# DLRM interaction tower on one core: rounds of sums over six units instead of four, with the dense features summed by TensorE

## The chip, the cores and the metric

The kernel runs on one core of one Trainium2 chip. The metric is the device time of an execution in microseconds (us).

## The reference, cut to what matters

512 examples look up one row of 64 floats in each of 40 tables. Each of the 780 pairs of fields has a 64 x 64 matrix, and gives one number per example. These 780 numbers and 16 dense features go through a small network.

```python
e = jnp.stack([tbl_0[ids[:, 0]], ..., tbl_39[ids[:, 39]]], axis=1)        # (512, 40, 64)
vi, vj = e[:, i_idx, :], e[:, j_idx, :]                                   # all pairs i < j, 780 of them
z = jnp.einsum('bpe,bpe->bp', jnp.einsum('bpd,pde->bpe', vi, W), vj)      # (512, 780)
h = jnp.concatenate([z, dense_ctx], axis=1)                               # (512, 796)
h = jnp.maximum(h @ W_top1 + b_top1, 0.0)                                 # 512 wide
h = jnp.maximum(h @ W_top2 + b_top2, 0.0)                                 # 256 wide
y = h @ W_top3
```

## The kernel before, in words

Everything is float32. The fields are kept in 20 pairs (NP), a pair on the 128 partitions of `x[:, k, :]`, 512 examples on the free axis. Sixteen pairs are gathered by GpSimd's indirect transfers (line 308) and turned by TensorE into bank `t_ps` (line 447, a "turn"); four pairs of small tables are looked up by TensorE with one-hot rows (line 429) that VectorE makes (line 385). ScalarE copies either into `x` (line 321).

The pairs of fields are worked through in 195 units (lines 64 to 74): 190 cross units (pair m with pair k, four matrices) and 5 inner units. For each unit s, in this order:

- TensorE (`multiply`, line 460) multiplies the unit's matrices with `x` into one of three slots of `y_ps` (Y_SLOTS; each slot is two banks): lines 477 for a cross unit, two products of 64 rows each, which run beside each other, and 483 for an inner one. It waits until VectorE has finished unit s - 3 (line 465). Each float32 matmul shows as two records.
- VectorE (`multiply`, line 394) multiplies both banks with the other pair of fields into `prod`, 128 x 1024 in one instruction (line 407). `prod` holds twelve units (G_UNITS); VectorE waits until the round that reads the old ones is done (line 396).
- TensorE (`sum_round`, line 488) sums the products over the 64 partitions of each half, and so makes rows of z: one matmul with a moved window of `selector` for each of a unit's two products, into one 32-partition quarter of the bank `z_ps` (line 500). Matmuls on different quarters run beside each other. A round takes ROUND = 4 units, eight products, two on each quarter, and is issued SUM_LAG = 3 units after its last unit. So the order on TensorE is: four units, a round, four units, a round. It waits for VectorE's last product of the round.
- After BANK_ROUNDS = 8 rounds `z_ps` is full with 128 rows (four more a round on each quarter) and ScalarE copies it to `z_sb` (line 337). There are seven such banks; the last gets one round of three units (`LAST_UNITS`).

Between the units stand jobs whose places are planned (`plan_jobs`, line 110): the turn of pair k goes three units before its first use, and two partial products of the first layer with banks 0 and 1, then 2 and 3 (line 456), four matmul groups each, spaced by six units and placed relative to ROUND and BANK_ROUNDS (line 120). All use the one bank `t_ps`. VectorE's one-hot rows for the last look-up are made at units 4, 7, 10 and 13 (ROWS_AT, line 47).

At the end TensorE begins the first layer with bank 4 (line 508), sums the last round, and goes on with banks 4, 5 and 6. The dense features are loaded early by a transfer straight into rows 4 to 19 of the last bank of `z_sb` (line 274; the rest of it is zeroed by VectorE at line 368), so ScalarE copies the last round in three pieces of four rows, one for each quarter in use (line 353), and leaves those rows standing. The second layer (line 538) and the last (line 544) follow.

SP issues the chunks of eight units' matrices, held back by the progress of the units (line 248), GpSimd's gathers are paced by it too (line 307).

Of the kernel before, what the change touches and what calls it, by code (L numbers as in the profile page):

```python
# [8 lines left out]
ACT = mybir.ActivationFunctionType  # L9
# [9 lines left out]
N_DENSE = 16  # L19
# [12 lines left out]
Y_SLOTS = 3  # L32
G_UNITS = 12
ROW_SLOTS = 6
ROUND = 4
BANK_ROUNDS = 8
SUM_LAG = 3
MIX_SLOTS = 2
LEAD = 3
# [38 lines left out]
STEPS = len(UNITS)  # L78
CHUNKS = -(-STEPS // CHUNK)
ROUNDS = -(-STEPS // ROUND)  # L80
BANKS = -(-ROUNDS // BANK_ROUNDS)
LAST_UNITS = STEPS - ROUND * BANK_ROUNDS * (BANKS - 1)
assert LAST_UNITS <= ROUND and STEPS == 195
FIRST_LATE = 2 * PARTIAL_PAIRS
DENSE_ROW = 4
INNER_AT = {u[1]: s for s, u in enumerate(UNITS) if u[0] == "inner"}


def pairs_of(s):

    unit = UNITS[s]
    if unit[0] == "cross":
        _, m, k = unit
        return [(h, h, hh, 2 * m + h, 2 * k + hh) for h in range(2) for hh in range(2)]
    a = 4 * unit[1]
    return [(n % 2, n // 2, n % 2 ^ n // 2, 2 * (a + n) + n % 2, 2 * (a + n) + 1 - n % 2) for n in range(4)]
# [5 lines left out]
    return slice(D * at, D * at + D)  # L102


def z_row(s, bank, half):
    r = s // ROUND
    return r // BANK_ROUNDS, 32 * (s % ROUND) + 4 * (r % BANK_ROUNDS) + 2 * bank + half


def plan_jobs():  # L110
# [8 lines left out]
    for pair in range(PARTIAL_PAIRS):  # L119
        start = ROUND * BANK_ROUNDS * 2 * (pair + 1) + SUM_LAG + 4  # L120
        for m in range(M1):
# [16 lines left out]
def round_at(s):  # L138
    r, rest = divmod(s - SUM_LAG - (ROUND - 1), ROUND)
    return r if rest == 0 and r >= 0 else None  # L140


def dlrm_tower(nc, ids, ids_one_hot, row_numbers, small_tables, tables, dense_t, w_units, w1, b1, w2, b2, w3, out):
    ctx = ExitStack()
    with ctx:
        def sb(name, shape, dt=F32):
            return ctx.enter_context(nc.sbuf_tensor(name, shape, dt))

        def ps(name, shape):
            return ctx.enter_context(nc.psum_tensor(name, shape, F32))  # L150

        def sem(name):
            return ctx.enter_context(nc.semaphore(name))

        ids_sb = sb("ids_sb", [P, BT, F], I32)
        ident = sb("ident", [P, P])
        selector = sb("selector", [P, 62])
# [5 lines left out]
        prod = sb("prod", [P, 2 * G_UNITS, B])  # L163
        z_sb = sb("z_sb", [P, BANKS, B])
# [22 lines left out]
        z_ps = ps("z_ps", [P, B])  # L187
        t_ps = ps("t_ps", [P, B])[:]

        def turn_ps(n):  # L190
            bank = TURN_BANK[n]
            return t_ps if bank == 2 * Y_SLOTS else y_ps[:, bank // 2, bank % 2, :]
# [13 lines left out]
        dense_loaded = sem("dense_loaded")  # L206
# [14 lines left out]
        round_summed = sem("round_summed")  # L221
        z_saved = sem("z_saved")
# [15 lines left out]
        def wait_x(eng, k):  # L238
            wait_turn_done(eng, TURN_SEQ["look" if k in ONE_HOT_PAIRS else "turn", k])
# [4 lines left out]
        def _(sp):  # L244
# [25 lines left out]
            for c in range(1, CHUNKS):  # L270
                load_weights(c)
                if c == 5:
                    sp.wait_ge(z_zeroed, 1)
                    sp.dma_start(z_sb[DENSE_ROW:DENSE_ROW + N_DENSE, BANKS - 1, :],
                                 dense_t).then_inc(dense_loaded, 16)
# [37 lines left out]
        @block.scalar  # L313
        def _(act):
            def copy_turn(job):
                n = TURN_SEQ[job]
                if job[0] == "partial" and job[1]:
                    return
                act.wait_ge(turned, n + 1)
                if job[0] in ("look", "turn"):  # L320
                    act.activation(x[:, job[1], :], turn_ps(n), ACT.Copy).then_inc(turn_on_act, 1)  # L321
                else:
                    act.activation(partial[job[2]], turn_ps(n), ACT.Copy).then_inc(turn_on_act, 1)

            def mix(q):
                if q >= MIX_SLOTS:
                    act.wait_ge(prod_ready, INNER_AT[q - MIX_SLOTS] + 1)
                for n in range(4):

                    k, into, other = 4 * q + n, D * (n % 2 ^ n // 2), D * (1 - n % 2)  # L330
                    wait_x(act, k)
                    act.activation(x_mix[into:into + D, q % MIX_SLOTS, n // 2, :], x[other:other + D, k, :],  # L332
                                   ACT.Copy).then_inc(mixed, 1)

            def save_bank(r):
                act.wait_ge(round_summed, r + 1)
                act.activation(z_sb[:, r // BANK_ROUNDS, :], z_ps[:], ACT.Copy).then_inc(z_saved, 1)  # L337

            for s in range(STEPS):
                for job in JOBS_AT[s]:  # L340
                    if job[0] == "mix":
                        mix(job[1])
                    else:
                        copy_turn(job)
                if (r := round_at(s)) is not None and r % BANK_ROUNDS == BANK_ROUNDS - 1:
                    save_bank(r)
            for r in range(BANK_ROUNDS - 1, ROUNDS, BANK_ROUNDS):
                if ROUND * r + ROUND - 1 + SUM_LAG >= STEPS:
                    save_bank(r)
            act.wait_ge(round_summed, ROUNDS)  # L350
            act.wait_ge(dense_loaded, 16)
            for c in range(LAST_UNITS):
                act.activation(z_sb[32 * c:32 * c + 4, BANKS - 1, :], z_ps[32 * c:32 * c + 4, :],
                               ACT.Copy).then_inc(z_saved, 1)
            act.wait_ge(mlp_loaded, 64)
            for m in range(M1):
                act.wait_ge(h1_added, m + 1)
                act.activation(h1_sb[:, m, :], partial[m], ACT.Relu, bias=b1_sb[:, m:m + 1]).then_inc(h1_ready, 1)
            for m in range(M2):
                act.wait_ge(h2_summed, m + 1)  # L360
                act.activation(h2_sb[:, m, :], h2_ps[m], ACT.Relu, bias=b2_sb[:, m:m + 1]).then_inc(h2_ready, 1)
            act.wait_ge(out_summed, 1)
            act.activation(y_sb, out_ps, ACT.Copy).then_inc(out_ready, 1)  # L363
# [57 lines left out]
        def _(pe):  # L421
# [66 lines left out]
            def sum_round(r):  # L488
                units = range(ROUND * r, min(ROUND * r + ROUND, STEPS))
                pe.wait_ge(prod_ready, units[-1] + 1)  # L490
                if r == 0:
                    pe.wait_ge(selector_ready, 2)
                elif r % BANK_ROUNDS == 0:
                    pe.wait_ge(z_saved, r // BANK_ROUNDS)
                row = 4 * (r % BANK_ROUNDS)
                for n in range(2):
                    for u in units:
                        last = n == 1 and (r % BANK_ROUNDS == BANK_ROUNDS - 1 or u + ROUND >= STEPS)
                        q = 32 * (u % ROUND)
                        ins = pe.matmul(z_ps[q:q + 32, :], selector[:, 30 - row - 2 * n:62 - row - 2 * n],  # L500
                                        prod[:, 2 * (u % G_UNITS) + n, :],
                                        start=(n == 0 and row == 0), stop=last)
                ins.then_inc(round_summed, 1)

            def first_layer(b, m):
                if m == 0:
                    pe.wait_ge(z_saved, b + 1 if b < BANKS - 1 else b + LAST_UNITS)
                return pe.matmul(h1_ps[m], w1_sb[:, b, P * m:P * m + P], z_sb[:, b, :],  # L508
                                 start=(b == FIRST_LATE), stop=(b == BANKS - 1))

            pe.wait_ge(ident_ready, 1)
            for s in range(STEPS):
                for job in JOBS_AT[s]:
                    if job[0] != "mix":
                        turn(job)
                multiply(s)
                if (r := round_at(s)) is not None:
                    sum_round(r)
# [10 lines left out]
            for b in range(FIRST_LATE, BANKS):  # L529
                for m in range(2 if b == FIRST_LATE else 0, M1):  # L530
                    ins = first_layer(b, m)
# [3 lines left out]
            for k in range(M1):  # L535
                pe.wait_ge(h1_ready, k + 1)
                for m in range(M2):
                    ins = pe.matmul(h2_ps[m], w2_sb[:, k, P * m:P * m + P], h1_sb[:, k, :],  # L538
                                    start=(k == 0), stop=(k == M1 - 1))
                    if k == M1 - 1:  # L540
                        ins.then_inc(h2_summed, 1)
            for k in range(M2):
                pe.wait_ge(h2_ready, k + 1)
                ins = pe.matmul(out_ps, w3_sb[:, k:k + 1], h2_sb[:, k, :], start=(k == 0), stop=(k == M2 - 1))  # L544
# [3 lines left out]
def pair_numbers():  # L548
    return {p: n for n, p in enumerate(zip(*np.triu_indices(F, k=1)))}
# [13 lines left out]
def lay_out_top1(w):  # L563
    number = pair_numbers()
    laid = np.zeros((P, BANKS, N1), w.dtype)
    for s in range(STEPS):
        for _, bank, half, i, j in pairs_of(s):
            z_bank, row = z_row(s, bank, half)
            i, j = ORDER[i], ORDER[j]
            laid[row, z_bank] = w[number[(min(i, j), max(i, j))]]  # L570
    laid[DENSE_ROW:DENSE_ROW + N_DENSE, BANKS - 1] = w[len(number):]
    return laid


# [35 lines left out]
```

## Time and profile before

| | |
|---|---|
| median of 3 runs | 365.91 us (365.79 to 366.19) |
| the profiled execution: its own time | 367.68 us |
| the profiled execution: span | 365.9 us |
| TensorE matmuls busy | 349.1 us (95%) |
| VectorE busy | 259.1 us (71%) |
| GpSimd busy | 153.9 us (42%) |
| ScalarE busy | 38.4 us (10%) |
| TensorE on the chain that ended last | 87% |

The span runs from the first to the last instruction in the trace. PE is TensorE's matmul, PEld its weight load, DVE VectorE, ACT ScalarE, SP SyncE. The chain of waits is followed back from the last instruction, at each step to what released it. L500 is line 500 of the kernel.

### The profile page before, as it was taken

What the parts mean: (1) busy time and instruction counts of PE and PEld (TensorE: products, weight loads), DVE (VectorE), ACT (ScalarE), POOL (GpSimd) and SP (SyncE); (2) the same over time, 40 slices, a digit from 0 to 9 for tenths busy, and PEclk for the clock granted to TensorE, in tenths of its full rate; (3) what the DMA queues carried; (4) which work ended last, traced back from release to release, by engine and by line L of the source; (5) the groups of instructions that cost most, each with busy time, mean ns of one, the idle gap of its engine ahead of it and who ended that gap; (6) DMA issues with size and microseconds to landing.
All of it is one profiled execution on the core that took longest, in us unless ns stands there. A gap on an engine that the chain in (4) does not pass through costs nothing.

```text
span 365.9 us, 4723 instructions
## 1 busy us (share of the span) xinstructions
PE 349.1 (95%) x1848; PEld 118.1 (32%) x1848; DVE 259.1 (71%) x271; ACT 38.4 (10%) x61; POOL 153.9 (42%) x261
## 2 busy tenths in 40 slices
PE   0989979999999999999999999999999999999997
PEld 0332223333323333333333333333333333333342
DVE  3956688378787787665768787887668687877430
ACT  1010300030100301010000300000000001200232
POOL 2888888337776754443534453253223000000000
PEclk9999989999999999999999999999999999999999
DMA  6961122002722222112202221122022000000000
GB/s 205 409 246 22 23 79 75 20 14 73 277 83 64 92 77 72 59 22 73 68 11 73 72 69 23 58 71 68 13 65 68 5 0 2 0 0 3 0 1 0
DMA packets 11448, 24.29 MB, mean 66 GB/s; under 512 B 3857, under 2 KB 3857, under 8 KB 11298
## 3 DMA queue, kind: packets, MB, share of 16 engines
q1 hardware_dynamic: 7330, 19.79, 15.4%
q0 software_dynamic: 4096, 4.20, 5.5%
q8 instruction: 14, 0.23, 0.3%
q14 instruction: 8, 0.07, 0.1%
HBM read 23.98 MB, written 0.00 MB: 66 GB/s over the span
## 4 chain that ended last, share of the span: by engine, by line
PE 87%; issue 8%; DVE 2%; DMA 1%; ACT 1%; SPq 0%; DVEq 0%
PE y_ps L477 45%; PE z_ps L500 24%; PE t_ps L456 4%; PE y_ps L508 3%; PE t_ps L447 2%; PE t_ps L429 2%; PE y_ps L429 2%; PE y_ps L538 2%; DVE one_hot L385 1%; DMA x<-in_ids_one_hot 1%; PE y_ps L483 1%; DVE prod L407 1%; ACT x L321 1%; PE t_ps L544 0%; ACT prod L363 0%
## 5 line engine op out<-in xcount | busy, mean ns | idle before, releaser
L407 DVE TENSOR_TENSOR prod<-y_ps,x 128x1024 f32<-128x1024 f32 x190 | 221.0, 1217 | 75.7 <-PE y_ps L477 74.4
L477 PE MATMUL y_ps<-x,w_sb 64*128 64x512 f32 x760 | 182.5, 610 | 4.9 <-ACT x L321 2.3
L308 POOL DMA_INDIRECT rows<-in_tbl,ids_sb x128 | 122.7, 958 | 129.6 <-PE y_ps L477 92.7
L477 PEld LDWEIGHTS y_ps<-x,w_sb 64*128 64x128 f32 x760 | 67.0, 186 | 109.3 <-issue 58.2
L500 PE MATMUL z_ps<-prod,selector 128*32 128x512 f32 x780 | 95.3, 604 | 0.0
L500 PEld LDWEIGHTS z_ps<-prod,selector 128*32 128x32 f32 x780 | 20.6, 110 | 67.9 <-issue 37.7
L429 PE MATMUL t_ps<-one_hot,table 128*64 128x512 f32 x96 | 22.8, 631 | 8.4 <-DVE one_hot L385 8.4
L385 DVE TENSOR_SCALAR one_hot<-x,numbers 128x512 f32<-128x512 int32 x64 | 27.2, 496 | 4.9 <-DMA x<-in_ids_one_hot 4.9
L303 POOL MEMSET spacer<- 128x128 f32 x127 | 30.5, 240 | 0.1
L321 ACT ACTIVATE x<-t_ps 128x512 f32<-128x512 f32 x18 | 10.8, 597 | 188.8 <-PE t_ps L447 149.9
L456 PE MATMUL t_ps<-z_sb,w_sb 128*128 128x512 f32 x32 | 15.9, 618 | 0.0
L429 PEld LDWEIGHTS t_ps<-one_hot,table 128*64 128x64 f32 x96 | 7.2, 146 | 22.8 <-issue 22.5
L332 ACT ACTIVATE x_mix<-x 64x512 f32<-64x512 f32 x20 | 12.6, 628 | 0.5
L337 ACT ACTIVATE z_sb<-z_ps 128x512 f32<-128x512 f32 x6 | 3.6, 597 | 80.5 <-PE z_ps L500 80.5
L508 PE MATMUL y_ps<-z_sb,w_sb 128*128 128x512 f32 x24 | 10.8, 601 | 0.0
L447 PE MATMUL t_ps<-ident,rows 128*128 128x128 f32 x60 | 9.8, 286 | 0.7 <-ACT x L321 0.7
L447 PEld LDWEIGHTS t_ps<-ident,rows 128*128 128x128 f32 x60 | 6.3, 140 | 12.8 <-issue 9.7
L418 DVE TENSOR_TENSOR partial_sb<-y_ps,partial_sb 128x512 f32<-128x512 f32 x3 | 2.1, 691 | 10.0 <-PE y_ps L508 10.0
L456 PEld LDWEIGHTS t_ps<-z_sb,w_sb 128*128 128x128 f32 x32 | 5.4, 189 | 10.2 <-issue 10.2
L429 PE MATMUL y_ps<-one_hot,table 128*64 128x512 f32 x32 | 7.0, 592 | 0.0
L538 PE MATMUL y_ps<-prod,w_sb 128*128 128x512 f32 x16 | 7.0, 592 | 0.0
L407 DVE TENSOR_TENSOR prod<-y_ps,x_mix 128x1024 f32<-128x1024 f32 x5 | 6.1, 1217 | 0.9 <-issue 0.9
(30 smaller groups left out, 36.1 us busy)
## 6 DMA issues: line engine op xcount, KB each, us to landing
w_sb<-in_w_units SPq DMA_DIRECT2D x25, 512.0 KB
x<-in_ids_one_hot SPq DMA_DIRECT2D x8, 256.0 KB, 4.9
table<-in_small_tables SPq DMA_DIRECT2D x8, 256.0 KB, 4.8
rows<-in_tbl,ids_sb POOLq DMA_INDIRECT x128
w_sb<-in_w SPq DMA_DIRECT2D x1, 1792.0 KB
w_sb<-in_w SPq DMA_DIRECT2D x1, 512.0 KB
ids_sb<-in_ids SPq DMA_DIRECT2D x1, 80.0 KB, 4.7
z_sb<-in_dense_t SPq DMA_DIRECT2D x1, 32.0 KB
```

Source lines behind the costliest of these rows:

```text
L303: pool.memset(spacer[:], 0.0).then_inc(spaced, 1)
L308: pool.indirect_dma_start(rows[:, n % ROW_SLOTS, bt, h * D:(h + 1) * D], None, tables[f], bass.IndirectOffsetOnAxis(ap=ids_sb[:, bt, f:f + ...
L321: act.activation(x[:, job[1], :], turn_ps(n), ACT.Copy).then_inc(turn_on_act, 1)
L385: ins = dve.tensor_scalar(one_hot[:, h, k, :], ids_all[:, 2 * n + h, :], numbers[:, k:k + 1], None, ALU.is_equal)
L407: dve.tensor_tensor(prod[:, at:at + 2, :], y_ps[:, s % Y_SLOTS], leaf, ALU.mult).then_inc(prod_ready, 1)
L429: ins = pe.matmul(dst[D * h:D * h + D, :], table[:, n, h, k, :], one_hot[:, h, k, :], start=(k == 0), stop=(k == TK - 1))
L447: ins = pe.transpose(dst[:, P * bt:P * bt + P], rows[:, at % ROW_SLOTS, bt, :], ident[:])
L456: ins = pe.matmul(dst, w1_sb[:, b, P * m:P * m + P], z_sb[:, b, :], start=(b % 2 == 0), stop=(b % 2 == 1))
L477: ins = pe.matmul(y_ps[:, slot, h, :], w_sb[own, c % W_SLOTS, at:at + P], x[own, m, :], start=True, stop=True)
L500: ins = pe.matmul(z_ps[q:q + 32, :], selector[:, 30 - row - 2 * n:62 - row - 2 * n], prod[:, 2 * (u % G_UNITS) + n, :], start=(n == 0 and ...
L508: return pe.matmul(h1_ps[m], w1_sb[:, b, P * m:P * m + P], z_sb[:, b, :], start=(b == FIRST_LATE), stop=(b == BANKS - 1))
L538: ins = pe.matmul(h2_ps[m], w2_sb[:, k, P * m:P * m + P], h1_sb[:, k, :], start=(k == 0), stop=(k == M1 - 1))
```

## The change

A round takes six units, twelve products, laid one after the other on the four quarters in three turns, each turn two rows further. A bank takes five rounds (120 rows), there are still seven banks, and 33 rounds in place of 49. The last round has three units. Its bank is now copied whole; the dense features, still loaded into `z_sb` (now rows 16 to 31), are first added into `z_ps`, on quarter 2, rows 16 to 31 of it, by one more matmul with 32 columns of the identity. The partials move from units 71, 77, 83, 89 and 135, 141, 147, 153 to 67, 73, 79, 85 and 127, 133, 139, 145. Y_SLOTS, G_UNITS and SUM_LAG stay. With ROUND = 6, the order on TensorE is six units, a round, six units, a round.

```diff
-ROUND = 4
-BANK_ROUNDS = 8
+ROUND = 6
+BANK_ROUNDS = 5
+QUARTERS = 4
+ROUND_ROWS = 4 * ROUND // QUARTERS
...
-LAST_UNITS = STEPS - ROUND * BANK_ROUNDS * (BANKS - 1)
-assert LAST_UNITS <= ROUND and STEPS == 195
+LAST_UNITS = STEPS - ROUND * (ROUNDS - 1)
+assert LAST_UNITS == 3 and STEPS == 195
...
-DENSE_ROW = 4
+
+DENSE_ROW = 16
+DENSE_QUARTER = 2 * LAST_UNITS % QUARTERS
...
+def place_of(u, bank):
+
+    return divmod(2 * u + bank, QUARTERS)
+
+
 def z_row(s, bank, half):
     r = s // ROUND
-    return r // BANK_ROUNDS, 32 * (s % ROUND) + 4 * (r % BANK_ROUNDS) + 2 * bank + half
+    turn, quarter = place_of(s % ROUND, bank)
+    return r // BANK_ROUNDS, 32 * quarter + ROUND_ROWS * (r % BANK_ROUNDS) + 2 * turn + half
...
-            act.wait_ge(round_summed, ROUNDS)
-            act.wait_ge(dense_loaded, 16)
-            for c in range(LAST_UNITS):
-                act.activation(z_sb[32 * c:32 * c + 4, BANKS - 1, :], z_ps[32 * c:32 * c + 4, :],
-                               ACT.Copy).then_inc(z_saved, 1)
+            save_bank(ROUNDS - 1)
...
-                row = 4 * (r % BANK_ROUNDS)
-                for n in range(2):
-                    for u in units:
-                        last = n == 1 and (r % BANK_ROUNDS == BANK_ROUNDS - 1 or u + ROUND >= STEPS)
-                        q = 32 * (u % ROUND)
-                        ins = pe.matmul(z_ps[q:q + 32, :], selector[:, 30 - row - 2 * n:62 - row - 2 * n],
-                                        prod[:, 2 * (u % G_UNITS) + n, :],
-                                        start=(n == 0 and row == 0), stop=last)
+                row = ROUND_ROWS * (r % BANK_ROUNDS)
+                for u in units:
+                    for n in range(2):
+                        turn, quarter = place_of(u % ROUND, n)
+                        first = row + 2 * turn
+                        if r == ROUNDS - 1:
+                            last = 2 * (u % ROUND) + n + QUARTERS > 2 * LAST_UNITS
+                        else:
+                            last = r % BANK_ROUNDS == BANK_ROUNDS - 1 and turn == 2 * ROUND // QUARTERS - 1
+                        ins = pe.matmul(z_ps[32 * quarter:32 * quarter + 32, :], selector[:, 30 - first:62 - first],
+                                        prod[:, 2 * (u % G_UNITS) + n, :], start=(first == 0), stop=last)
+                if r == ROUNDS - 1:
+                    pe.wait_ge(dense_loaded, 16)
+                    ins = pe.matmul(z_ps[32 * DENSE_QUARTER:32 * DENSE_QUARTER + 32, :], ident[:, 0:32],
+                                    z_sb[:, BANKS - 1, :], start=False, stop=True)
                 ins.then_inc(round_summed, 1)
 
             def first_layer(b, m):
                 if m == 0:
-                    pe.wait_ge(z_saved, b + 1 if b < BANKS - 1 else b + LAST_UNITS)
+                    pe.wait_ge(z_saved, b + 1)
```

The rows of the first layer's weights are laid out on the host to match.

## Rows read from the trace of the kernel before

**Rows 1.** Busy time by stretch: stretch, length, PE, PEld, DVE, ACT, POOL, PEclk, DMA.

```profile
48.70:52.50 3.80, 3.80 (x16) 0.87 (x20) 3.80 (x7) 0.00 (x0) 2.99 (x6) 0.55 0.10 17
...
69.09:342.48 273.39, 273.36 (x1537) 91.98 (x1537) 210.23 (x183) 23.19 (x38) 102.58 (x175) 1.00 0.18 53
```

**Rows 2.** Chain of waits, middle: start us, us, engine, tile, line, records.

```profile
192.44 3.63 PE y_ps L477 x16
196.08 1.85 PE z_ps L500 x16
...
226.32 1.92 PE y_ps L477 x8
228.24 0.58 PE t_ps L447 x4
...
249.06 1.91 PE t_ps L456 x4
...
308.09 1.06 PE y_ps L477 x4
```

**Rows 3.** Timeline, 161 to 169 us: start, us, engine, line, records, [idle before <-releaser].

```profile
161.24 1.13 PE L477 MATMUL y_ps<-x,w_sb 64*128 64x512 f32 x4
...
165.80 3.70 PE L477 MATMUL y_ps<-x,w_sb 64*128 64x512 f32 x16
...
167.05 4.62 DVE L407 TENSOR_TENSOR prod<-y_ps,x 128x1024 f32<-128x1024 f32 x4 [1.69 <-PE y_ps L477]
...
168.33 0.35 PEld L477 LDWEIGHTS y_ps<-x,w_sb 64*128 64x128 f32 x4 [0.51 <-DVE prod L407]
```

**Rows 4.** Timeline, 113 to 121 us, where VectorE is behind.

```profile
113.04 8.01 DVE L407 TENSOR_TENSOR prod<-y_ps,x 128x1024 f32<-128x1024 f32 x7 [1.65 <-PE y_ps L477]
...
115.05 3.79 PE L477 MATMUL y_ps<-x,w_sb 64*128 64x512 f32 x16
...
117.71 0.30 PEld L477 LDWEIGHTS y_ps<-x,w_sb 64*128 64x128 f32 x4 [0.64 <-DVE prod L407]
```

**Rows 5.** Timelines of PE, then of DVE, 40 to 70 us.

```profile
40.76 1.09 PE L483 MATMUL y_ps<-x,w_sb 64*64 64x512 f32 x8
41.78 1.93 PE L500 MATMUL z_ps<-prod,selector 128*32 128x512 f32 x16
43.64 3.31 PE L477 MATMUL y_ps<-x,w_sb 64*128 64x512 f32 x12
48.68 1.70 PE L477 MATMUL y_ps<-x,w_sb 64*128 64x512 f32 x4 [1.74 <-DVE prod L407]
50.30 3.00 PE L500 MATMUL z_ps<-prod,selector 128*32 128x512 f32 x16
...
61.22 7.09 PE L429 MATMUL t_ps<-one_hot,table 128*64 128x512 f32 x32
69.09 1.13 PE L477 MATMUL y_ps<-x,w_sb 64*128 64x512 f32 x4 [0.79 <-ACT x L321]
...
42.28 2.34 DVE L407 TENSOR_TENSOR prod<-y_ps,x 128x1024 f32<-128x1024 f32 x2
...
47.41 3.47 DVE L407 TENSOR_TENSOR prod<-y_ps,x 128x1024 f32<-128x1024 f32 x3
...
52.44 1.20 DVE L407 TENSOR_TENSOR prod<-y_ps,x 128x1024 f32<-128x1024 f32 x1
55.90 2.36 DVE L407 TENSOR_TENSOR prod<-y_ps,x 128x1024 f32<-128x1024 f32 x2 [2.26 <-PE y_ps L477]
58.18 1.78 DVE L385 TENSOR_SCALAR one_hot<-x,numbers 128x512 f32<-128x512 int32 x4
```

**Rows 6.** Chain of waits at the end.

```profile
344.39 1.85 PE z_ps L500 x12
346.24 8.78 PE y_ps L508 x20
```

**Rows 7.** Groups of instructions on ScalarE: busy us, mean ns, idle before.

```profile
L353 ACT ACTIVATE z_sb<-z_ps 4x512 f32<-4x512 f32 x3 | 1.8, 587 | 3.2 <-PE z_ps L500 3.2
```

More of the change, by code:

```diff
@@ L570, in lay_out_top1 @@
             laid[row, z_bank] = w[number[(min(i, j), max(i, j))]]
-    laid[DENSE_ROW:DENSE_ROW + N_DENSE, BANKS - 1] = w[len(number):]
+    dense_row = 32 * DENSE_QUARTER + DENSE_ROW
+    laid[dense_row:dense_row + N_DENSE, BANKS - 1] = w[len(number):]
     return laid
```

## The prediction, made before the changed kernel ran

> **What bounds the kernel now.** I read the stages first [rows 1]. From 69.09 us to 342.48 us TensorE has no gap: 273.36 of 273.39 us busy at granted clock 1.00, the higher of its two levels (2.4 GHz), while VectorE works 210.23 us. So this middle, three quarters of the time, is TensorE's. Then the chain of waits [rows 2]: it stays on TensorE and falls into pieces of a few fixed lengths. Units in a run: 1.06 us for one, 1.92 for two, 3.63 for four, so 0.857 us each, and the first of a run 0.205 more. A round of sums over four units (two turns of four quarters) takes 1.85 us: two turns of 0.855 (two passes at the pace of the units' passes) and 0.14 fixed. A turn of gathered rows takes 0.58 to 0.59, a partial first layer 1.91 to 1.92. Last, how close VectorE stands behind it [rows 3]: its first product starts 1.25 us after the first weight load of a run (165.80 to 167.05), it takes 1.22 us, and four end 4.62 us after the first began, so they follow each other by 1.13. TensorE's load for the run's fourth unit went at 168.33, 0.06 after that first product had ended (168.27): there are only three y_ps slots. From a load to the end of its unit's matmuls are 1.13 us (the run of one unit). The fourth unit would by itself end 3.70 after the start and can end at 2.53 + 1.13 = 3.66 by the slot: four units fit with 0.04 to spare. That margin is the whole case.
>
> **Rounds and restarts.** 49 rounds become 33; in the middle stretch, where order and counts follow from the planner, 45 become 30. A round of twelve products in three turns takes 0.14 + 3 x 0.855 = 2.705 us. The turns set it, not the products: the last round, with twelve records on three quarters, took 1.85 as the sixteen on four did [rows 6, 2]. 45 x 1.85 = 83.25 becomes 30 x 2.705 = 81.15: 2.10 less. Runs of cross units (each ended by a round, a turn, a partial or an inner unit) fall from 60 to 52, as many of the new ones are still cut by a job: 8 x 0.205 = 1.64 less. As a check, the old counts (175 cross units at 0.857, 60 restarts, 4 inner units at 1.02, 13 turns, 8 partials, 45 rounds) give 272.6 us against 273.4 in the trace; the rest is a few late VectorE starts, which I leave in. Sum: **3.74 us less** if nothing waits.
>
> The fixed 0.14 and 0.205 are where a mode of TensorE changes. The Trainium skill ("TensorEngine Tiling (Array Packing)", Key Properties) says that changing the tiling mode drains the engine; by that rule fewer rounds are a plain gain. The same page (PSUM Bottleneck) warns that tiling speeds up TensorE but not the emptying of PSUM, which may become the bottleneck. That speaks against this change, and the next step is its case in rows.
>
> **The wait that comes.** Six units now follow each other. From the first load of the run, and with VectorE idle as it is there: units 0 to 3 end at 1.13, 1.99, 2.84, 3.70. VectorE starts at 1.25, 2.39, 3.52, 4.65 and ends 1.22 later: 2.47, 3.61, 4.74. The load of unit 4 waits for the second product: 3.67, and the unit ends at 4.80, not 4.56 (0.24 late). Unit 5 waits for the third: load at 4.80, end at 5.93. By itself it would end at 5.41: **0.515 us lost per uninterrupted six**. The round behind takes 2.705, VectorE is through at about 8.15, the next run starts at 8.56, so nothing carries over and each such run pays again. That this is how a late slot is paid the trace shows once [rows 4]: seven products back to back (8.01 us), a weight load at 117.71, 0.06 after a product, and the run ends at 118.84, 1.13 behind the load, 0.09 later than four units by themselves. By the order of the new plan the middle has 11 uninterrupted sixes (5.67), three runs of five cross units (0.24 each) and three bursts where an inner unit sits within the six (0.15 each): **6.83 us more**. The other bursts are cut after at most four units by a turn (with the restart 0.8 us) or a partial (2.1), in which VectorE catches up; those cost nothing. VectorE's fresh idle time is not work and costs nothing by itself. Bounds of this term: 5.7 (each uninterrupted six 0.1 us cheaper, twice the 0.04 to 0.06 to which rows 3 fix a step) to 7.6 (the 0.75 us of late starts met once more, in runs without slack).
>
> **The beginning** [rows 5]. Here VectorE's one-hot rows are on the chain. Before, round 0 (41.78) stands ahead of unit 7, whose slot was free only at 43.55 anyway; units 7, 8, 9 end at 46.94, and TensorE then waits 1.74 us for a product. Round 1 comes at 50.30, at a lowered clock, before turn and unit 11, and so VectorE's unit 11 starts only at 55.90 after 2.26 us of idleness. After: units 7 and 8 end at 45.9, round 0 (2.7) fills the wait, unit 9 ends at 49.6 against 48.5 to 49.7 that VectorE wants; unit 10 at 50.5, the turn at 51.1 (it waited for no gather before, at 53.23), and unit 11 can start at 51.8, behind the copy of that turn (some 0.78 us, as before unit 16 at 69.09). VectorE's unit 11 then follows unit 10 directly at 53.6, its one-hot rows of step 13 (from 58.18 before) are done by 57.6, and units 13 to 15 and round 1 end by 59.7. The look-up starts at 59.6 instead of 61.22, unit 16 at 67.5 instead of 69.09: **1.6 us less**. The clock is the doubt: it was 0.55 from 48.7 to 52.5 [rows 1], behind the 1.74 us of waiting [rows 5], and stretched round 1 from 1.93 to 3.00 and unit 10 from 1.13 to 1.70. After, TensorE waits as long, but from 41.85 (the inner unit's end) to 43.55, and is then dense. If it falls all the same it lands on round 0 and unit 9, delays them by some 1.5 us and the gain is gone. Bounds: 0 to 2.1 less. I take 1.6, as what comes right behind the wait is now denser.
>
> **The end.** The last round has six products and the dense one, on quarters 0, 1, 2, 3, 0, 1 and 2: two turns, 1.85 us as before [rows 6]. Should the dense product not run beside the others, 0.86 more; I take 0. ScalarE's three copies of 4 rows (0.587 us each, [rows 7]) become one; they lay beside the first layer's twelve passes ahead of bank 6 (some 5.1 of the 8.78 us, [rows 6]), so 0 again. Cover gone, they would have cost 1.8. The dense wait is for a transfer issued near the sixth weight chunk, over long before. Partials move 4 to 8 units forward; w1 has landed long before, bank 1 is copied five units ahead. ScalarE and the SP and POOL queues issue the same, paced by the same units. Products have twelve slots: unit 12 needs round 0, which is issued behind unit 8, so VectorE doesn't wait there.
>
> **Sum:** -3.74 + 6.83 - 1.6 = +1.5 us. The profiled execution has a span of 365.9 us and its own time was 367.68; I set the change against its span and put it on the median of the runs, 365.91: 367.4. A measurement of this kernel can tell about 0.2% (0.73 us) from no change.
>
> **The rivals.**
> (a) The clock falls in the beginning again: +3.1, 369.0. For it: the same length of waiting. Against: the round now stands right behind. 0.2.
> (b) The other side, faster: the run of six doesn't wait, since the load for unit 4 and 5 overlaps the product before it or VectorE starts each run earlier. Then -3.74 - 1.6: 360.6. It decides where the waits sum to less than 4.6 us of my 6.83. Against it stand rows 3 and 4, where load follows product by 0.06 and end follows load by 1.13. By the drain rule of the Trainium skill ("TensorEngine Tiling (Array Packing)", Key Properties) alone this would be the result. 0.1.
> (c) The change doesn't do what it says: the third turn isn't as cheap as the second, with another 0.14 or so of start for each of 30 rounds: +4.2 more, 371.6. Rows 2 and 6 give no sign. 0.05.
> (d) Smaller errors in both terms cancel and leave nothing to measure: waits at 5.7 and the beginning at 2.1 give 365.8. 0.1.
> The forecast itself has 0.55, of which 0.04 ends within 0.73 us of no change and 0.02 below.
>
> **How the numbers follow.** Likeliest 367.4. The range leaves out (b), (c) and the edges: from 365.4, just below (d), to 369.8, which is (a) with the waits at 7.6. Slower: the forecast's 0.49, (a) and (c), 0.74. Same: (d) and the forecast's 0.04, 0.14. Faster: (b) and 0.02, 0.12.
>
> **What would show it.** Chain: sum rounds of 24 records at 2.70; runs of six at 5.86 in place of 5.34 (0.52 more), with loads of y_ps released by VectorE at units 4 and 5, 0.06 after a product; runs of four before a partial at 3.63. The idle time of VectorE grows, though its work is the same. Unit 16 at about 67.5 and no stretch at 0.5 clock, or a stretch on round 0, which would be (a). The end from 342 on keeps its 23.4 us. Runs of six at 5.34 would make the prediction wrong toward (b), rounds over 2.8 toward (c).

## The result, and the profile after

The changed kernel takes 370.4 us (median of 6, 369.2 to 371.03), the kernel before 366.05 us beside it (median of 6): ratio 1.0111, interval 1.0089 to 1.0133. It is slower, as forecast, but by 4.35 us where 1.5 were forecast, and it lies outside the range (365.4 to 369.8). One execution of the kernel before, of 1247 us, is left out of everything below.

Its profiled execution has a span of 367.3 us, 1.4 more than that of before. That looks like the forecast and isn't: the two profiles are of different kinds of execution. Either kernel has executions whose granted clock is 1.00 on the mean and others with 0.995. Each profile of the second kind (seven, of these two kernels and of variants) has one stretch at the lower level (1.2 GHz), which lies between 43 and 54 us. The profile of before was of that kind [rows 1], that of after of the first. Over all comparisons of this study in which the span is on record:

| | clock 1.00 | clock 0.995 |
|---|---|---|
| before | 48 executions, mean 364.05 us | 32 executions, mean 365.5 us |
| after | 8 executions, mean 367.8 us | 10 executions, mean 369.65 us |

So the loss is 3.8 us against the same kind at 1.00 and 4.1 at 0.995, and a median also depends on how many executions of each kind it holds. Device time is 1.75 to 2.13 us above the span in all 80 executions of before, and in 16 of the 18 of after; in the other two, both of this first comparison, it is 2.31 and 3.12 above.

Busy time by stretch of the kernel after (columns as in [rows 1]): the middle, from unit 16 to the first layer, and the place where before had its clock stretch.

```profile
67.75:343.94 276.19, 275.90 (x1537) 92.22 (x1537) 208.97 (x183) 23.81 (x39) 102.94 (x177) 1.00 0.16 52
48.70:52.50 3.80, 3.02 (x16) 1.38 (x18) 3.80 (x7) 0.60 (x1) 2.98 (x6) 1.00 0.12 26
```

The middle is 2.8 us longer than the 273.39 of [rows 1]; that one held 0.3 us of late VectorE starts, and the undisturbed middle of before is 273.0 (below). In the experiments the middle ends with the first record of the first layer, 0.07 us earlier than in this line; by that it is 276.12 here. Its chain of waits, to set beside [rows 2]:

```profile
180.04 3.63 PE y_ps L483 x16
183.68 0.59 PE t_ps L453 x4
184.27 1.92 PE y_ps L483 x8
186.18 2.71 PE z_ps L510 x24
...
197.45 4.72 PE y_ps L483 x20
202.17 0.09 issue
202.26 1.13 PE y_ps L483 x4
203.39 2.71 PE z_ps L510 x24
...
242.88 3.63 PE y_ps L483 x16
246.52 1.91 PE t_ps L462 x4
```

A round of twelve products takes 2.71 us, the sum's 2.705. Four units ahead of a turn or a partial take 3.63 here, as before, and up to 3.71 elsewhere. An uninterrupted six takes 4.72 + 0.09 + 1.13 = 5.94 here and in one other place, and 5.84 to 5.88 in nine, where six by themselves would be 5.34. Over the eleven the waits come to 5.7 us, and 5.67 was worked out. The timeline of that run, to set beside [rows 3]:

```profile
197.38 6.01 PE L483 MATMUL y_ps<-x,w_sb 64*128 64x512 f32 x24
...
198.63 5.75 DVE L413 TENSOR_TENSOR prod<-y_ps,x 128x1024 f32<-128x1024 f32 x5 [1.68 <-PE y_ps L483]
...
201.04 0.30 PEld L483 LDWEIGHTS y_ps<-x,w_sb 64*128 64x128 f32 x4 [0.78 <-DVE prod L413]
...
202.23 0.33 PEld L483 LDWEIGHTS y_ps<-x,w_sb 64*128 64x128 f32 x4 [0.89 <-issue]
```

VectorE begins 1.25 us after the first load, as before. The load of unit 4 went at 201.04, 3.66 after the start of the run (3.67 was worked out), and that of unit 5 at 202.23, 4.85 after it (4.80 worked out). The row calls the second gap "issue", but the load goes 0.12 behind the end of the third product (198.63 + 1.22 + 2 x 1.13 = 202.11).

The beginning, to set beside [rows 5]: PE's timeline of the kernel after.

```profile
40.77 1.09 PE L489 MATMUL y_ps<-x,w_sb 64*64 64x512 f32 x8
43.58 2.35 PE L483 MATMUL y_ps<-x,w_sb 64*128 64x512 f32 x8 [1.72 <-DVE prod L413]
45.86 2.78 PE L510 MATMUL z_ps<-prod,selector 128*32 128x512 f32 x24
48.57 1.99 PE L483 MATMUL y_ps<-x,w_sb 64*128 64x512 f32 x8
50.49 0.66 PE L453 MATMUL t_ps<-ident,rows 128*128 128x128 f32 x4
51.92 4.25 PE L483 MATMUL y_ps<-x,w_sb 64*128 64x512 f32 x16 [0.78 <-ACT x L331]
56.10 2.78 PE L510 MATMUL z_ps<-prod,selector 128*32 128x512 f32 x24
58.81 1.13 PE L483 MATMUL y_ps<-x,w_sb 64*128 64x512 f32 x4
59.87 7.09 PE L435 MATMUL t_ps<-one_hot,table 128*64 128x512 f32 x32
```

The wait for VectorE of 1.74 us ahead of unit 10 has become one of 1.72 ahead of unit 7. Units 11 to 14 take 4.18 (51.92 to 56.10) where four take 3.63, as VectorE is still behind. The end (chain of waits), beside [rows 6]:

```profile
343.94 1.91 PE y_ps L521 x4
345.85 1.41 PE z_ps L510 x10
347.26 0.01 PE z_ps L514
347.27 0.42 PE z_ps L510 x2
347.69 0.01 PE z_ps L514
347.70 8.78 PE y_ps L521 x20
```

The last round with the dense product (line 514) takes 1.85 us in sum, as forecast. The dense product's two records show as 0.01 us each: it runs beside the others. From the first layer on, both kernels take 23.4 us.

### The profile page after: what moved, and what is told of

The parts are those of the page before. It is cut to its first block, busy times and chain, and to the rows that moved or that the text cites. A ratio compares the mean times of both kernels' runs of the same rounds, so it can differ in the third digit from the quotient of the medians.

```text
span 367.3 us, 4724 instructions
## 1 busy us (share of the span) xinstructions
PE 350.7 (95%) x1850; PEld 118.3 (32%) x1850; DVE 258.1 (70%) x271; ACT 37.2 (10%) x59; POOL 154.0 (42%) x261
## 4 chain that ended last, share of the span: by engine, by line
PE 90%; POOL 3%; DMA 3%; issue 2%; ACT 1%; DVE 1%; SPq 0%; DVEq 0%
PE y_ps L483 49%; PE z_ps L510 24%; PE t_ps L462 4%; PE t_ps L435 4%; PE y_ps L521 3%; PE t_ps L453 2%; POOL rows L318 2%; PE y_ps L551 2%; DMA rows<-in_tbl,ids_sb 2%; DMA ids_sb<-in_ids 1%; PE y_ps L489 1%; POOL spacer L313 1%; ACT x L331 1%; PE t_ps L557 0%; DVE one_hot L391 0%
## 5 line engine op out<-in xcount | busy, mean ns | idle before, releaser
L483 PE MATMUL y_ps<-x,w_sb 64*128 64x512 f32 x760 | 186.3, 613 | 5.2 <-ACT x L331 2.3
L483 PEld LDWEIGHTS y_ps<-x,w_sb 64*128 64x128 f32 x760 | 65.6, 185 | 115.3 <-issue 61.1
L510 PE MATMUL z_ps<-prod,selector 128*32 128x512 f32 x780 | 90.9, 596 | 0.0
L510 PEld LDWEIGHTS z_ps<-prod,selector 128*32 128x32 f32 x780 | 22.1, 109 | 63.9 <-issue 55.6
```

The costliest lines, as they stand in the source:

```text
L483: ins = pe.matmul(y_ps[:, slot, h, :], w_sb[own, c % W_SLOTS, at:at + P], x[own, m, :], start=True, stop=True)
L510: ins = pe.matmul(z_ps[32 * quarter:32 * quarter + 32, :], selector[:, 30 - first:62 - first], prod[:, 2 * (u % G_UNITS) + n, :], start=(f ...
```

## The experiments

### The kernel before again

No edit.

> The kernel before, unchanged, to see span and clock of each execution. Theory (atypical profile): the profile of before held a clock stretch at 0.5 that most of its executions don't have; then most spans are near 364.0 us at granted clock 1.00, and one with 0.995 is near 365.9. In a profile without the stretch unit 16 starts near 67.5 us in place of 69.09. Rival (the stretch is always there, and the changed kernel loses outside what its profile shows): all spans near 365.9 at 0.995.

Measured: 367.38 us against 366.17 for the runs beside it; ratio 1.0014, interval 0.9997 to 1.003. Spans of its own executions: 363.5, 363.9, 363.9 at clock 1.00 and 365.5 to 365.8 at 0.995, eight times. Of the executions beside it, 17 of 23 were at 1.00. The theory holds in that there are two kinds, 1.5 us apart. That most are of the first kind holds over all (48 of 80) and not in this run's own eleven. Its profile had the stretch again, so the profile without one comes from the next run.

### The new layout and the dense product with rounds of four

```diff
-ROUND = 6
-BANK_ROUNDS = 5
+ROUND = 4
+BANK_ROUNDS = 8
```

> The changed kernel with rounds of four units and eight rounds a bank: only the new laying on the quarters, the dense product in the last round and the whole copy of the last bank are left of the change. Theory: the last round stays at 1.85 us and the time is that of the kernel before within 0.3 us. Rival (the dense product or the copy is on the path): 0.4 to 0.9 us slower, with the last round at 2.3 to 2.7.

Measured: 366.19 us against 366.17, ratio 0.9996, interval 0.9981 to 1.0012. The layout, the dense product and the whole copy cost nothing and bring nothing. As its order of work is that of the kernel before, its profile at clock 1.00 also shows what that of before would have been. PE's timeline and the busy time of the middle:

```profile
41.20 1.09 PE L489 MATMUL y_ps<-x,w_sb 64*64 64x512 f32 x8
42.22 1.92 PE L510 MATMUL z_ps<-prod,selector 128*32 128x512 f32 x16
44.22 3.39 PE L483 MATMUL y_ps<-x,w_sb 64*128 64x512 f32 x12
49.27 1.13 PE L483 MATMUL y_ps<-x,w_sb 64*128 64x512 f32 x4 [1.66 <-DVE prod L413]
50.33 1.92 PE L510 MATMUL z_ps<-prod,selector 128*32 128x512 f32 x16
```

```profile
68.04:341.06 273.02, 272.99 (x1536) 91.97 (x1536) 210.22 (x183) 23.17 (x38) 102.57 (x175) 1.00 0.18 53
```

Unit 10 takes 1.13 and round 1 takes 1.92 us, where [rows 5] have 1.70 and 3.00: 1.65 us less, with nothing changed in the order. Executions begin up to 1 us apart, so I count from the inner unit: unit 16 starts 26.84 us behind it here (68.04 - 41.20), 28.33 in the profile of before (69.09 - 40.76) and 26.98 in that of after (67.75 - 40.77). The changed order itself gains nothing in the beginning; it loses 0.14 us.

### VectorE's products cut to three quarters, before and after

Both kernels with KEPT = 384: VectorE leaves out the products of the last 128 of the 512 examples.

```diff
-dve.tensor_tensor(prod[:, at:at + 2, :], y_ps[:, s % Y_SLOTS], leaf, ALU.mult)
+dve.tensor_tensor(prod[:, at:at + 2, 0:KEPT], y_ps[:, s % Y_SLOTS, :, 0:KEPT], leaf, ALU.mult)
```

> The kernel before with VectorE's products cut to 384 of the 512 examples (the last 128 of prod are zeroed once at the start, so their output is wrong): its pace falls from 1.13 to about 0.87 us a unit, TensorE's work is as before. Theory (VectorE doesn't bind in runs of four): the middle stretch, from unit 16 to the first layer, keeps its 273.4 us within 0.8; in all at most 2 us faster by the beginning. Rival (VectorE already holds back the runs of four): the middle gains over 2 us.

> The changed kernel with the same cut of VectorE's products to 384 of 512 examples (same part of the output wrong). Theory (each uninterrupted run of six waits 0.5 us for a y_ps slot): the waits vanish, runs of six go from 5.84 to 5.34 us, the middle stretch goes from 276.2 to 269 or 270 us, and this kernel is 3 to 4.5 us faster than the kernel before with the same cut, so the sign of the change turns. Rival (the longer run is slow for another reason, on TensorE itself): runs of six stay at 5.8, and it stays 2 to 4 us slower than the kernel before with the cut.

Measured: 363.78 us with rounds of four (ratio to the kernel before 0.9918, interval 0.9897 to 0.9939) and 360.77 us with rounds of six (0.9835, 0.9814 to 0.9856). The middle stretches of the two (first line: four; second: six), and a run of six between rounds from the second kernel's chain:

```profile
65.92:338.64 272.72, 272.72 (x1537) 93.14 (x1537) 163.96 (x183) 23.14 (x38) 104.33 (x179) 1.00 0.18 53
```

```profile
66.73:335.78 269.05, 269.05 (x1537) 95.58 (x1537) 163.18 (x183) 23.81 (x39) 103.74 (x177) 1.00 0.18 54
```

```profile
183.14 2.71 PE z_ps L514 x24
185.85 5.35 PE y_ps L487 x24
191.20 2.71 PE z_ps L514 x24
```

This settles the main cause. With a quicker VectorE the middle of rounds of four stays (272.7 against 273.0), that of rounds of six falls by 7.1 us, runs of six take 5.35, and six is then 3.67 us better than four in the middle, where 3.74 were worked out for rounds and restarts. The waits for a slot cost the difference, 276.12 - 269.05 = 7.1 us; 6.83 were forecast. The kernel as a whole becomes 3 us faster than its partner: the sign turns.

The same two profiles bear on the clock. The wait in the beginning is shorter in both, and all eight executions are at clock 1.00:

```profile
47.15 1.13 PE L481 MATMUL y_ps<-x,w_sb 64*128 64x512 f32 x4 [0.73 <-DVE prod L411]
```

```profile
43.37 2.08 PE L487 MATMUL y_ps<-x,w_sb 64*128 64x512 f32 x8 [0.93 <-DVE prod L417]
```

### The changed kernel again

No edit.

> The changed kernel, unchanged, to set its executions with a clock stretch beside those without one. Theory (two kinds of execution, in both kernels): spans near 367.5 us at granted clock 1.00 and near 368.8 at 0.995, each 3.2 to 3.5 above the same kind of the kernel before (364.1 and 365.5); a profile with the stretch has it between 41 and 53 us, on the wait ahead of unit 7 or on round 0, and unit 16 starts 1.2 to 1.7 us later, with the middle stretch unchanged at 276.2. Rival (the change brings a loss of its own in some executions): the slower kind loses its time after 75 us.

Measured: 372.3 us, ratio 1.0148 (1.0118 to 1.0178); spans 368.7 and 369.2 at 1.00, 370.4 to 371.0 at 0.995. The clock stretch is where it was expected. PE's timeline of the profile, and the granted clock (column before the last two):

```profile
43.95 3.68 PE L483 MATMUL y_ps<-x,w_sb 64*128 64x512 f32 x8 [1.64 <-DVE prod L413]
47.56 2.78 PE L510 MATMUL z_ps<-prod,selector 128*32 128x512 f32 x24
```

```profile
36.00:52.50 16.50, 13.30 (x69) 4.65 (x68) 11.15 (x15) 3.71 (x6) 13.51 (x23) 0.90 0.22 55
69.60:347.20 277.60, 276.43 (x1536) 92.01 (x1536) 209.20 (x183) 23.81 (x39) 102.59 (x175) 1.00 0.17 52
```

Units 7 and 8, right behind the wait, take 3.68 where 2.35 stood above. But on this chip the middle is longer too, 277.6, and the spans at 1.00 are 1.4 us above those of the first comparison. In its timeline four VectorE products between 88 and 116 us begin 0.3 to 0.4 us later than their unit and the product before allow. The three runs of units behind them take 4.65, 5.02 and 6.21 us where the first profile has 3.86, 4.72 and 5.85: 1.45 us, the whole of what the middle is longer. So there is a third, smaller part.

### Turns and partials right behind a round

The kernel before, with its jobs at other units (turn of pair 10 at unit 43 in place of 44, and so on):

```diff
+TURN_AT = {7: 19, 8: 27, 9: 35, 10: 43, 11: 51, 12: 63, 13: 75, 14: 91, 15: 103, 16: 119, 17: 135, 18: 151, 19: 171}
+PARTIAL_AT = ((71, 79, 83, 87), (139, 143, 147, 155))
-        jobs_at[FIRST[k] - LEAD].append(("turn", k))
+        jobs_at[TURN_AT[k]].append(("turn", k))
```

> The kernel before with turns and partials moved to right behind a round of sums (turns up to three units earlier, partials at units 71, 79, 83, 87 and 139, 143, 147, 155), so that they don't cut a run of four. Theory (a restart of a run costs 0.205 us, and runs of four wait for nothing): with 13 restarts less in the middle that is 2.6 us off the middle stretch, 273.4 to 270.8, and off the time. Rival (the cuts gave VectorE the time it needs, or the restart is hidden): under 1 us.

Measured: 364.54 us, ratio 0.9939 (0.9919 to 0.9959); spans 361.85 on the mean at 1.00 and 363.4 at 0.995, six executions each. The middle:

```profile
69.00:339.60 270.60, 270.57 (x1536) 92.66 (x1536) 209.19 (x183) 23.19 (x38) 102.59 (x175) 1.00 0.18 53
```

Work and rounds are the same; 13 restarts at 0.205 us are 2.67, and the middle fell from 273.0 to 270.6. A job that doesn't split a run is cheaper.

### Rounds of two units

```diff
-ROUND = 6
-BANK_ROUNDS = 5
+ROUND = 2
+BANK_ROUNDS = 16
```

The last round has one unit, and the mark of the last product on a quarter is set to match.

> The changed kernel with rounds of two units, one turn of the four quarters each, sixteen rounds a bank: 98 rounds, as many turns of the quarters as in every version. Theory (a round costs 0.14 us and a restart 0.205 beside its turns, and short runs wait for nothing): a round is 0.995 us, the middle stretch 287 us, in all 13.6 us (13 to 14.5) slower than the kernel before. Rival (a round's fixed part is paid by turn or by product, or hidden in the wait for VectorE): under 8 us slower.

Measured: 379.81 us, ratio 1.0368 (1.0334 to 1.0402). The chain of waits:

```profile
192.45 0.99 PE z_ps L511 x8
193.44 1.92 PE y_ps L483 x8
195.36 1.00 PE z_ps L511 x8
```

One turn of the quarters with its start is 0.99 to 1.00 us, two units with their restart 1.92: both fixed parts stand as worked out. The middle is 288.0 us; by span the whole is 13.8 us longer than before at clock 1.00 (377.8 against 364.05). The theory holds.

### Turns placed to cut the runs of six

The changed kernel with the turns of eight pairs (nine, says the expectation) moved up (8: 23, 10: 41, 12: 59, 13: 69, 15: 95, 17: 129, 18: 149, 19: 161, the rest as they were).

> The changed kernel with nine of the turns moved up to eleven units earlier, to where they cut an uninterrupted run of six: the same work and the same number of jobs in other places. Theory (only uninterrupted runs of over four wait for VectorE): the waits in the middle fall by some 4 us, restarts rise by some 2, so it is 2.2 us (1.5 to 2.8) faster than the changed kernel, near the kernel before. Rival (the loss doesn't hang on where the jobs stand): within 0.7 us of the changed kernel.

Measured: 370.17 us, ratio 1.0101 (1.0062 to 1.014). Against the changed kernel in the same comparison, on the same chip, the median is 2.1 us lower (372.3), and the spans are 1.8 lower at either clock (367.2 against 368.95; 368.9 against 370.7). Against the changed kernel's spans in the first comparison, on a chip that isn't on record, they are only 0.4 lower (367.5). Its profiled middle is 276.3, no shorter than the changed kernel's, but six VectorE products began late there, by 2.6 us together, the largest 0.96. Two runs of units took all of it, one of them this:

```profile
112.05 2.85 PE L484 MATMUL y_ps<-x,w_sb 64*128 64x512 f32 x12
115.62 3.30 PE L484 MATMUL y_ps<-x,w_sb 64*128 64x512 f32 x12 [0.73 <-DVE prod L414]
```

These six units take 6.81 us to the next round, where others take 5.85; four units from 86.32 on take 5.32, where the changed kernel has 3.86. Without these 2.4 us the middle would be 273.9, 2.2 less than 276.12, and 2.2 were forecast. That is an estimate from one profile, and the executions at one clock are three against two: they favour the theory over its rival (within 0.7 us), and don't prove it.

### The late gathers left out, before and after

```diff
-            for n, k in enumerate(GATHERED):
+            for n, k in enumerate(GATHERED[:ROW_SLOTS]):
```

> The kernel before with the gathers of the last ten gathered pairs left out (their turns take what stands in the six slots of rows, so the output is wrong); TensorE, VectorE and ScalarE do what they did. Control for the next run. Late starts of VectorE (a product that begins later than 0.117 us behind its unit and behind its last product) came in profiles between 84 and 128 us, while the gathers run densely. Theory (gathers cause them, and runs of four absorb most): the late starts there are gone, spans stay within 0.4 us of 364.1 at granted clock 1.00 and of 365.5 at 0.995.

> The changed kernel with the same gathers left out (same part of the output wrong). Theory (gathers make VectorE start late, and runs of six have no room for it, which is what the executions lose beyond the 3.1 us of the middle): spans are within 0.4 us of 367.3 at granted clock 1.00 and of 368.8 at 0.995, not spread up to 369.2 and 371.0, and the distance to the kernel of the run before falls to 3.1 to 3.5 us. Rival (the spread has another source): spans still reach 369 at 1.00 and 370.5 at 0.995, distance 4 or more.

Measured: 366.75 us (ratio 1.0005, 0.9985 to 1.0024) and 368.81 us (1.0069, 1.0042 to 1.0096). Spans: before, 364.1 on the mean at 1.00 and 365.65 at 0.995; after, 366.9 to 367.2 (five) and 368.5, 369.2. That is 2.9 and 3.2 us apart, the middle's 3.1, and no spread. It looked like the theory, but both were on another chip than the changed kernel's slowest comparison; the last one below takes it up.

### The wait filled

The changed kernel:

```diff
                 unit, c = UNITS[s], s // CHUNK
+                if s == 7:
+                    for _ in range(2):
+                        pe.matmul(t_ps, ident[:], x[:, 0, :], start=True, stop=True)
```

> The changed kernel with two idle-filling matmuls (identity by x into the free bank t_ps, result unused) ahead of unit 7, where TensorE waits 1.7 us for VectorE. Theory (the clock falls in some executions because of that wait): no execution at 0.995 is left, all spans are those of granted clock 1.00 (367.3 to 369.2), and the mean falls by about 1 us. Rival (the clock falls for another cause, such as the waits of units 8 and 13 to 14): about half of the executions still at 0.995.

Measured: 369.51 us, ratio 1.0077 (1.005 to 1.0103). All six executions are at clock 1.00, spans 366.9 to 367.8. PE's timeline:

```profile
41.15 1.98 PE L470 MATMUL t_ps<-x,ident 128*128 128x512 f32 x4
43.07 2.24 PE L486 MATMUL y_ps<-x,w_sb 64*128 64x512 f32 x8
```

The two matmuls (line 470) end about when the wait would have ended, and the clock no longer falls. The theory holds for the cause of the stretch: of the changed kernel's executions 10 of 18 are at 0.995, here none of six.

### Both kernels beaten: jobs behind the rounds, and the wait filled

The kernel of the moved jobs, with the same two matmuls ahead of unit 10 (`if s == 10`).

> The kernel before with the jobs right behind the rounds (as in the run with the moved jobs) and two idle-filling matmuls ahead of unit 10, where TensorE waits 1.74 us. Theory: the restarts saved (2.4 to 2.7 us) and no clock stretch: all spans near 361.7 us at 1.00, so 363.6 us of device time, 2.5 to 3 us faster than the kernel before. Rival: the stretch stays, half of the spans are near 363.2.

> The kernel before with aligned jobs and the filled wait, again, for its interval on a second chip: 363.3 us, 2.5 to 3 us faster than the kernel before, no execution at 0.995.

Measured: 363.34 us, ratio 0.991 (0.9887 to 0.9934), and on a second chip 363.53, ratio 0.9936 (0.9913 to 0.9958). All twelve executions at clock 1.00, where the same kernel without the filling had six of twelve at 0.995. The beginning and the middle:

```profile
36.00:52.50 16.50, 15.09 (x80) 5.01 (x80) 13.19 (x20) 3.57 (x7) 13.51 (x23) 1.00 0.21 56
67.39:337.80 270.41, 270.38 (x1536) 92.74 (x1536) 208.97 (x183) 23.15 (x38) 103.42 (x177) 1.00 0.18 53
```

### Chip or gathers

Both kernels unchanged from above, on one chip.

> The changed kernel, unchanged, beside the next run on one chip. Theory (late starts while gathers run cost it about 1 us on average): spans at granted clock 1.00 spread from 367.0 to over 368, with a mean 0.5 us or more above that of the next run. Rival (chip or start of the execution): the means of the two at the same clock agree within 0.3 us.

> The changed kernel without the gathers of the last ten gathered pairs (their part of the output wrong), again. Theory: spans at 1.00 between 366.9 and 367.4, whatever the chip. Rival: they move up with those of the run before.

Measured: 370.25 us (1.0107, 1.0083 to 1.0131) and 369.83 us (1.0111, 1.0086 to 1.0137). Spans at 1.00: 366.9, 367.8, 367.4 with the gathers, 367.4, 367.4, 367.4, 366.9 without. The means agree within 0.1 us: the rival is right here, and the gathers cost nothing on this chip. Both profiled middles are 276.1 us. The changed kernel's extra loss came in one of its three comparisons; on that chip the gathers were never left out, and what makes VectorE start late there stays open.

## Why the prediction was wrong

**What bounds the kernel, rounds and restarts: right.** The middle without late starts is 273.0 us before and 276.1 after: 3.1 more, and 6.83 - 3.74 = 3.09 was worked out. The waits themselves are 7.1 and not 6.83, mostly by runs of four that were put at nothing and wait up to 0.08 us. Both terms stand on their own too: 3.67 us saved where nothing waits (VectorE at three quarters), 7.1 us of waits with VectorE at its pace. Rival (b), that the run of six doesn't wait, is refuted by the 5.84 to 5.94 us of the runs, rival (c) by the 2.71 us of the rounds. Of the two rules that stood beside the sum, the one of the Trainium skill ("TensorEngine Tiling (Array Packing)", PSUM Bottleneck) pointed the right way: emptying PSUM by VectorE decides, though VectorE is busy for only 209 of 276 us. The other, a drain at each change of mode, agrees with the traces as far as they go: 0.14 and 0.205 us stand where the mode changes, and having them less often was worth 3.7. That they are a drain no run separates.

**The end: right.** 0 was taken, 0 was measured (0.9996).

**The beginning: this step failed.** The term of -1.6 us is 69.09, where unit 16 started in the profile of before, less 67.5, where it would start after. The second number was good: the inner unit starts at the same time in both profiles (40.76 and 40.77), unit 11 was put at 51.8 and came at 51.92, unit 16 at 67.5 and came at 67.75. The first number was wrong as a baseline. It holds the clock stretch, and the text itself has its size: unit 10 from 1.13 to 1.70 and round 1 from 1.93 to 3.00, 1.64 us. At clock 1.00 both are that much shorter without any change of the order, and then the changed order gains nothing and loses 0.14. The lowered clock was weighed only as a doubt about the changed kernel. Nor did round 0 fill idle time on balance: the wait ahead of unit 10 (1.74, 1.66 at clock 1.00) went, and one of 1.72 came ahead of unit 7.

**The baseline: the same fault once more.** The text gives the profiled execution's own time, 367.68, and the median, 365.91, and puts a change read from the one on the other. The 1.8 us between them was the sign: the profiled execution was one of the slower 40 in 100, and a cost that it alone has must not be taken off a median that doesn't hold it. With the term at +0.1 the same sum gives 365.9 + 3.1 + 0.1 = 369.1 us.

**Rival (a)** (369.0, the clock falls again) came near in its number, and not for its reason. The clock falls in 10 of 18 executions of the changed kernel and in 32 of 80 of the kernel before. It is no cost that the change brings or takes; it is in both, some 1.5 us each time it comes, and hangs on the wait of some 1.7 us ahead of units 7 and 10. Rival (d), that nothing is left to measure, fell by the same term as the forecast: the waits were worth more than its 5.7 us and the beginning nothing.

**The rest.** From 369.1 to the 370.4 measured, 1.3 us remain. By span at clock 1.00 the first comparison lost 3.5 us (367.5 against 364.05), 0.2 or 0.3 more than the 3.24 of middle and beginning. Three of its six executions were at 0.995, which lifts the median of the spans by another 0.7. The 2.31 and 3.12 us outside the span in two of them lift the median by 0.3; what they are no run shows. In the last comparison the loss at the same clock was 3.3 and 3.45 us. In the one between it was 4.8 and 5.2, and 1.5 of that, in its profile, are late VectorE starts whose cause wasn't found.

## What to carry to other kernels

A producer with n slots ahead of a slower consumer can run on for n units and a little; make the run longer and it waits, even if the consumer is idle a quarter of the time. Check a longer batch against the slots, unit by unit, and put other jobs where they don't split a run that fits.

Before a profile is used as the baseline, set its own time against the median: if they differ by more than the effect in question, find what the profiled execution had that the others don't, and take it out of every term.

## What the runs showed of the hardware beyond that

With a wait of some 1.7 us of TensorE the granted clock fell to 1.2 GHz in 10 of 18 and 32 of 80 executions of the same program, and not in the rest. The length alone doesn't tell the two apart: profiles with the fall have waits of 1.64 to 1.93 us, profiles without it 1.66 to 1.72. With VectorE at three quarters, where the wait was 0.73 and 0.93 us, none of eight executions fell. Two matmuls of no use in the wait ended the falls in all 18 executions of three runs. The Trainium skill ("TensorE: Matmul & The Clock Gate", Part 1) lets the engine's activity decide between the two levels; the filled waits agree.
